# Causal attention of a six-layer decoder: values and ones in one weight tile, denominators out of the same matmul, squares moved on ScalarE

## The reference, cut to what matters

```
def _L1_attn_ref(x, g1, Wq, Wkv, Wout, g2):        # HEADS 16, DIM_HEAD 64, n = 128
    xn = layernorm(x, g1)
    q = xn @ Wq.T                                   # 16 heads of 64
    k, v = split(xn @ Wkv.T)                        # one key and one value head for all
    q, k = l2norm(q * 16) * 4, l2norm(k) * 4
    sim = einsum('bhid,bjd->bhij', q, k); causal mask
    attn = softmax(sim)
    out = einsum('bhij,bjd->bhid', attn, v) @ Wout.T
    return layernorm(out, g2)
x = _layernorm(x + _L1_attn_ref(...))
```

## Time and profile before

| | |
|---|---|
| median of three runs | 3569.23 us (3564.8 to 3569.68) |
| the profiled execution | 3576.01 us |
| its span, first to last instruction | 3574.3 us |
| mean granted clock of TensorE | 0.952 |
| PE busy | 3130.4 us (88%) |
| ScalarE busy | 2001.0 us (56%) |
| VectorE busy | 1776.5 us (50%) |
| GpSimd busy | 1151.1 us (32%) |
| `causal_phase` in the span | about 1851 to 2756 us |

### The profile page before, as it was taken

The page is one execution under the profiler, slowest core; times in us unless marked ns, Lnnn a source line. Parts: engine busy times, 40 slices in busy tenths (PEclk is TensorE's granted clock), DMA queues, the critical chain, the costliest instruction groups (busy, mean ns, idle before and its releaser), DMA issues. The chain is left out here.

```text
span 3574.3 us, 44153 instructions
## 1 busy us (share of the span) xinstructions
PE 3130.4 (88%) x12438; PEld 1667.9 (47%) x12438; DVE 1776.5 (50%) x2639; ACT 2001.0 (56%) x3736; POOL 1151.1 (32%) x954
## 2 busy tenths in 40 slices
PE   3777777779999999976669999999998879999997
PEld 1333333247777777742224444444444634444443
DVE  2888888835555555559963333343333321111110
ACT  2666666636666666635557777777775523233322
POOL 2777767712222222236643333333332000000000
PEclk8898899979999999989889999999999989999999
DMA  5333433300000000001100000000000310000001
GB/s 209 115 123 116 129 121 122 118 21 18 21 16 21 21 16 21 19 24 44 52 35 11 13 15 16 13 13 18 13 13 26 124 40 18 21 23 18 18 21 59
DMA packets 100808, 167.55 MB, mean 47 GB/s; under 512 B 11520, under 2 KB 42384, under 8 KB 100240
## 3 DMA queue, kind: packets, MB, share of 16 engines
q1 hardware_dynamic: 100752, 166.88, 13.8%
HBM read 81.57 MB, written 4.72 MB: 24 GB/s over the span
## 5 line engine op out<-in xcount | busy, mean ns | idle before, releaser
L1356 POOL TENSOR_TENSOR d_pr<-d_pr,d_keep 128x512 f32<-128x512 f32 x256 | 320.1, 1271 | 566.8 <-ACT d_pr L1514 566.8
L771 POOL TENSOR_TENSOR b_pn<-b_e,b_inv 128x616 f32<-128x616 f32 x128 | 161.3, 1260 | 603.1 <-DVE b_inv L952 603.1
L261 POOL TENSOR_TENSOR a_bx<-a_bcopy,a_drive_u 128x512 f32<-128x512 f32 x256 | 319.9, 1266 | 19.1 <-DVE a_state L524 18.5
L524 DVE TENSOR_TENSOR_SCAN a_state<-a_decay,a_bx 128x512 f32<-128x512 f32 x256 | 310.9, 1214 | 1.7 <-POOL a_bx L261 1.3
L281 PE MATMUL a_py<-a_prod,consts 128*128 128x512 f32 x512 | 299.3, 670 | 3.8 <-DVE a_t L504 3.1
L453 ACT ACTIVATE a_decay<-a_delta,neg_a 128x508 f32<-128x508 f32 x256 | 174.4, 683 | 146.2 <-DVE a_state L524 145.9
L1909 PE MATMUL f_ph<-f_hb,wb 128*128 128x512 f32 x512 | 232.8, 599 | 6.3 <-ACT f_hb L1944 6.3
L1909 PE MATMUL f_ph<-f_ha,wb 128*128 128x512 f32 x512 | 230.2, 599 | 2.3 <-DVE f_ha L1973 2.3
L293 PE MATMUL a_pc<-a_bc,sel 96*128 96x512 bf16 x256 | 110.1, 430 | 128.1 <-DVE a_prod L530 126.6
L927 DVE TENSOR_REDUCE b_peak<-b_pscore 128x8 f32<-128x616 f32 x128 | 102.2, 799 | 214.4 <-PE b_pscore L808 214.4
L877 ACT ACTIVATE b_yy<-b_py,y_bias 128x154 f32<-128x154 f32 x512 | 169.0, 381 | 66.4 <-PE b_py L817 66.2
(11 more groups left out here) (282 smaller groups left out, 6576.7 us busy)
## 6 DMA issues: line engine op xcount, KB each, us to landing
a_bcopy<-rows SPq DMA_DIRECT2D x256, 256.0 KB, 3.3
wb<-in_wb SPq DMA_DIRECT2D x1, 6714.0 KB, 34.5
x<-in_x SPq DMA_DIRECT2D x1, 4096.0 KB
a_xf<-x SPq DMA_DIRECT2D x16, 256.0 KB, 3.8
a_xt<-x SPq DMA_DIRECT2D x16, 256.0 KB, 2.3
x<-a_xo SPq DMA_DIRECT2D x16, 256.0 KB, 3.7
b_xf<-x SPq DMA_DIRECT2D x32, 128.0 KB, 2.0
b_xt<-x SPq DMA_DIRECT2D x32, 128.0 KB, 2.0
```

Of the source, the lines that this page charges most:

```text
L261: gp.tensor_tensor(bx[:, k % 4, :], bcopy[:, k % 4, :], drive_u[:, p, :], ALU.mult).then_inc(*bxt.step("bx"))
L524: V.tensor_tensor_scan(state[:, j % 2, :], decay[j % 2][:], bx[:, j % 4, :], 0.0, ALU.mult, ALU.add).then_inc(*vs.step("scan"))
L771: gp.tensor_tensor(heads(pn[:, j % 2, :]), heads(e[:, j % 2, :]), over(inv[:, j % 2, :], CTX), ALU.mult).then_inc(*pnt.step("n"))
L1356: gp.tensor_tensor(half, half, keep[:].unsqueeze(1).to_broadcast([128, QP, SEQ]), ALU.mult).then_inc(*gmt.step(f"m{odd}"))
```

## The change

The values tile `vv` becomes three blocks wide, ones, values, ones, for each sequence (one GpSimd memset of the whole tile to 1, then the values are copied into the middle block). `weighted` now is two matmuls that use all 128 output columns: for the even heads the weights are the blocks values, ones, for the odd heads ones, values. So `pattn` is two banks wide: the even heads' bank has values on partitions 0 to 63 and sums on 64 to 127, the odd heads' bank the other way round; `pden` and `ones` are gone. The logarithm of the sums is now two instructions of 64 partitions, each reading one half of the partitions and writing the other half of `den`, and so is the final product on VectorE (two instructions, of which the second raises the semaphore). ScalarE's `squares` no longer stand in the slots of `LENGTH` (but for slot 3) but in the odd slots of `QUERY`, the slot of their projection, between the logarithms and the exponential of the sums. The tables, the other engines' order and the waits are as they were. The lines below are numbered by the kernel after the change where they have a +.

```diff
--- before.py
+++ after.py
@@ -1236,8 +1236,7 @@
 
         kn = sb("kn", [128, 2, N])
         qn = sb("qn", [128, 2, PAIRS, N])
-        vv = sb("vv", [128, 2, NB, DH])
-        ones = sb("ones", [128, DH])
+        vv = sb("vv", [128, 2, NB, 3, DH])
         keep = sb("keep", [128, SEQ])
         shift = sb("shift", [128, 1])
         pr = sb("pr", [128, 2, 2, QP * SEQ])
@@ -1248,8 +1247,7 @@
         t3 = sb("t3", [128, N])
 
         pscore = ps("pscore", 1024)
-        pattn = ps("pattn")
-        pden = ps("pden")
+        pattn = ps("pattn", 1024)
         pq = [ps("pq0"), ps("pq1")]
         pn = ps("pn")
         pm = ps("pm")
@@ -1338,7 +1336,7 @@
             @block.gpsimd
             def _(pool):
                 gp = nc.gpsimd
-                gp.memset(ones[:], 1.0).then_inc(*made.step("ones"))
+                gp.memset(vv[:], 1.0).then_inc(*made.step("ones"))
                 gp.memset(shift[:], 0.5 * SHIFT * float(np.log(2.0))).then_inc(*made.step("shift"))
                 gp.memset(keep[:], 1.0).then_inc(*made.step("full"))
                 pool.wait_ge(*made.at("full", 0))
@@ -1381,10 +1379,9 @@
                         pe.wait_ge(*vat.at("n", r - 1))
                     if j == 0:
                         pe.wait_ge(*vf.at("v", g))
-                    for bank, w in ((pattn, vv[:, p, b, :]), (pden, ones[:])):
-                        for odd in range(2):
-                            op = mm(bank[64 * odd:64 * odd + 64, :], w, pr[:, j % 2, odd, :], start=True, stop=True,
-                                    skip_group_check=True)
+                    for odd in range(2):
+                        w = vv[:, p, b, 1 - odd:3 - odd, :].rearrange("p i d -> p (i d)")
+                        op = mm(pattn[:, 512 * odd:512 * (odd + 1)], w, pr[:, j % 2, odd, :], start=True, stop=True)
                     op.then_inc(*pea.step("a"))
 
                 def project(gu, pu, i, r, bank):
@@ -1490,8 +1487,9 @@
                         if k != 4:
                             if u := piece(UNIT, g, p, k, front, main):
                                 roots(*u)
-                        if u := piece(LENGTH, g, p, k, front, main):
-                            squares(*u)
+                        if k == 3:
+                            if u := piece(LENGTH, g, p, k, front, main):
+                                squares(*u)
                         if front and k == 0:
                             act.wait_ge(load, 16 * g + 32)
                             if begun(g):
@@ -1513,12 +1511,20 @@
                             for odd in range(2):
                                 A(pr[:, j % 2, odd, :], pscore[:, 512 * odd:512 * (odd + 1)], ACT.Exp, scale=16.0
                                   ).then_inc(*ext.step(f"e{odd}"))
-                        if u := summed(g, p, k, main, tail):
-                            _, _, j, r = u
+                        done = summed(g, p, k, main, tail)
+                        if done:
+                            _, _, j, r = done
                             act.wait_ge(*pea.at("a", r))
                             if begun(r - 1):
                                 act.wait_ge(*vat.at("n", r - 1))
-                            A(den[:], pden[:], ACT.Ln).then_inc(*sdt.step("ln"))
+                            for odd in range(2):
+                                op = A(den[64 * odd:64 * odd + 64, :],
+                                       pattn[64 - 64 * odd:128 - 64 * odd, 512 * odd:512 * (odd + 1)], ACT.Ln)
+                            op.then_inc(*sdt.step("ln"))
+                        if k % 2:
+                            if u := piece(QUERY, g, p, k, front, main):
+                                squares(*u)
+                        if done:
                             act.wait_ge(*sdt.at("ln", r))
                             A(den[:], den[:], ACT.Exp, scale=-1.0).then_inc(*sdt.step("inv"))
                         if k == 4:
@@ -1566,7 +1572,7 @@
                             dve.wait_ge(*pef.at("v", g + 1))
                             if begun(g - 1):
                                 dve.wait_ge(*pea.at("a", UNITS * g - 1))
-                            V.tensor_copy(vv[:, q, :, :], pn[:, 0:NB * DH].rearrange("p (b d) -> p b d", b=NB)
+                            V.tensor_copy(vv[:, q, :, 1, :], pn[:, 0:NB * DH].rearrange("p (b d) -> p b d", b=NB)
                                           ).then_inc(*vf.step("v"))
                         if u := piece(LENGTH, g, p, k, front, main):
                             gu, pu, i, r, bank = u
@@ -1581,10 +1587,13 @@
                             gu, pu, j, r = u
                             hh, b = j // 2, j % 2
                             dve.wait_ge(*sdt.at("inv", r))
-                            V.tensor_tensor(attn[:, pu, QP * hh:QP * (hh + 1), SEQ * b:SEQ * (b + 1)],
-                                            pattn[:].rearrange("p (i t) -> p i t", i=QP),
-                                            den[:].rearrange("p (i t) -> p i t", i=QP), ALU.mult
-                                            ).then_inc(*vat.step("n"))
+                            for odd in range(2):
+                                half = slice(64 * odd, 64 * odd + 64)
+                                op = V.tensor_tensor(
+                                    attn[half, pu, QP * hh:QP * (hh + 1), SEQ * b:SEQ * (b + 1)],
+                                    pattn[half, 512 * odd:512 * (odd + 1)].rearrange("p (i t) -> p i t", i=QP),
+                                    den[half, :].rearrange("p (i t) -> p i t", i=QP), ALU.mult)
+                            op.then_inc(*vat.step("n"))
                         if tail and k == 4:
                             dve.wait_ge(*so.at("rstd", g - 1))
                             SC(out=t1[:], in0=pm[:, 0:N], scalar=W["g2"], in1=t3[:], op0=ALU.mult, op1=ALU.mult
```

## The result

The changed kernel takes 3605.6 us (median of four runs, 3603.6 to 3612.0) against 3569.5 (four runs): ratio 1.0104, 95% interval [1.0088, 1.0120]. It is 36 us slower. The forecast was 3574 with a range of 3548 to 3588; the measured time is outside it, beyond the slower rival D too.

A forecast was written before the change was run, and what follows sets the result against it. PE was taken as the bound, ScalarE and VectorE close behind. Loop +3.5, first turn -1.1 and last full step +2.7 made +5.1 us on the profiled 3576.0, forecast 3574 against the median 3569.2, range 3548 to 3588.

The forecast's parts named there:

- rival D: Halves do not overlap: second logarithm costs 0.60, second product 0.69; +0.38 us per step, 3586 us; chance 0.20.
- What bounds the kernel: PE, busy 26.75 of 27.42 us per step; ScalarE and VectorE half a microsecond behind in one half.
- The change of the array's shape: On PE, whole-array neighbours save each `weighted` 0.35 us of switching, 1.4 us per step; no streaming is saved.
- The price of the halves: Second logarithm on ScalarE adds 0.49 us, second product on VectorE 0.61, the pitches of instructions that need not wait.
- Steps 3 to 6 of the replay: Slots 5 to 1: `weighted` of slot 7 waits for the product, ending 18.52; L1430 waits for L1599, ending 23.14.
- The bounds: The range 3548 to 3588 leaves out B and half of C at the bottom, the end of D at the top.
- signs of being wrong: PE shows no wait for `d_xo`, a half instruction is shorter than 0.5 us, or the period is below 27.
- signs of being right: Gapless `weighted` of 1.72 us, second product ending 3.4 after first logarithm's start, PE waits for `d_attn` and `d_xo`, 27.5 us steps.
- B: PE stays the bound, through half-price halves or slack in the chain: -1.42 us per step, 3527 us; chance 0.10.
- C: The chain decides at `weighted` but not at L1430: step 26.78 us, near 3550 us; chance 0.12.
- The sum: Loop 29 x 0.12 = +3.5 us, first turn -1.1, last full step +2.7; together +5.1.

The follow-up runs named there:

- single_evac: The changed kernel with weights of ones and only one logarithm and one product, on 128 partitions of the first bank (computes something else): 3528.9 us, ratio 0.9881.
- squares_only: The kernel before with only ScalarE's squares moved between logarithm and exponential of the sums: 3560.6 us, ratio 0.9971.
- out_first: The changed kernel with VectorE's `d_xo` moved ahead of the two halves of the attention product in slot 7: 3592.1 us, ratio 1.0062.
- no_swap: The changed kernel with weights of ones, each half logarithm reading the partitions it writes (computes something else): 3604.9 us, ratio 1.0097.

## Why the prediction was wrong, point by point

- **What bounds the kernel.** Right: PE with ScalarE and VectorE close behind in slots 4 to 0. The change made these two the bound.
- **The change of the array's shape.** Right in size (no streaming saved, the gaps gone; `single_evac` and the rows after). Its 1.4 us per step would be worth 1.0 on top of `squares_only`, since the scores then wait.
- **The price of the halves: the step that failed.** The prediction put it so: "length does not follow partitions; what counts is the pitch of two that need not wait for each other: 0.49 on ScalarE ... and 0.61 on VectorE. I take these." The first clause held (0.59 and 0.69 us on 64 partitions). The pitches were read from instructions that start at partition 0. Measured: logarithm to logarithm 0.605, logarithm to squares 0.61, product to product 0.70, product to `d_xo` 0.725, root to logarithm 0.746 instead of 0.629 in the kernel before. Along the chain: 0.12 at the root of slot 5, then in each of the two rounds 0.25 on ScalarE (1.71 from logarithm to exponential instead of 1.46) and 0.09 on VectorE, and 0.12 at `d_xo`: 0.92 us, where the step measured, 28.46, is 0.92 over the step forecast, 27.54. With 128-partition pitches the chip gave 27.47. That the sum closes to the hundredth is luck: two misses of 0.06 cancel. The exponentials of slot 4 started at 8.91 instead of 8.85, and L1427 followed `d_xo` by 0.06 instead of 0.12. The 0.12 was itself misread: the rows named for it give 0.14.
- **Steps 3 to 6 of the replay.** The places and their order held: `weighted` of slots 5 and 7 waits for `d_attn`, L1427 (L1430 before) for `d_xo`, 1.27 us where 1.1 was forecast. Counted from the scores of slot 2, `weighted` of slot 7 ended at 19.03 instead of 18.52, and L1427 at 24.06 instead of 23.14. The wait of lengths was 0.37 us on average where 0.2 was forecast.
- **The bounds and rival D.** D had the right mechanism, halves that do not overlap, and made it 0.38 us per step. It took the lack of overlap between the two halves only and not with the neighbours on both sides, which is more than half of the 0.92. So the end of the range, 3588, was no bound.
- **The signs.** None of the three signs of being wrong came: PE waits for `d_xo`, a half takes 0.59 us, the period is over 27. They guarded against a faster kernel only. Of the signs of being right, the one that failed points at the step that did: the second product ends 3.76 us after the start of the first logarithm, not 3.4.
- **B and C.** B needed halves at half price or slack in the chain; neither is there. C's chain, which decides at `weighted`, is what `out_first` has: 27.91 us per step.
- **The sum.** Loop: some 30 steps of 1.08 make 32 us; the phase as a whole is 35.8 us longer, the rest lies in the steps written out at its start and end. The forecast of their part, 1.6 us, was too small by about 2.

The rule of the Trainium skill that a change of tiling mode drains TensorE ("TensorEngine Tiling (Array Packing)", Key Properties) was borne out by the missing gaps and was not what decided. The rows, all of instructions that start at partition 0, could not show what a change of the starting partition costs.

## What to carry to other kernels

Before a full-width instruction is split by partitions, price each part at its full length plus the overlap lost on both sides, unless a trace shows that very form overlapping, with the same starting partitions in the instructions around it. Then follow the chain that the parts stand in to the next wait of the bounding engine: a gain on PE (1.4 us per step here) is worth only what the queue that hands its banks back can follow. And read the waits of PE's weight loads beside those of its matmuls.

## What the runs showed of the hardware that was not expected

Two independent instructions in a row on ScalarE or VectorE overlap by 0.07 to 0.13 us, on 128 or 64 partitions, on ScalarE also on 77, when all of them start at partition 0. When an operand starts at another partition than the last operand before it in the same memory, the next instruction starts 0.01 to 0.03 us after the end instead: 0.09 to 0.12 us lost per boundary. This was seen on both engines for changes between 0 and 64, ahead of a half that starts at 64 and behind it. On ScalarE the last read of PSUM counts even with an instruction between that reads SBUF alone (`no_swap`, two places). A half instruction on 64 x 512 elements takes 0.59 us on ScalarE and 0.69 us on VectorE, as long as a whole one.
